# Output rows made token by token: nine products in one bank, attention's last, and the bias added to the input rows by GpSimd

## What is computed

```python
# x: (4, 1024, 128), 16 heads of 8; everything in float32
xn = layernorm(x)
attn = softmax(causal(rope(q) @ rope(k).T / sqrt(8))) @ v          # q, k, v = xn @ Wqkv
y = attn @ Wproj                                                   # "proj"
# product-key experts: per token 4 heads, 8 best of 8 x 8 pairs out of 512 experts
w = silu(xn @ down_embed[idx]) * softmax(scores)                   # as a dense (tokens, 512) matrix "coef"
experts = w @ up_embed
mlp = (silu(xn @ Wg + bg) * (xn @ Wu + bu)) @ Wd + bd
out = x + y + experts + mlp
```

## Time and profile before

| | us |
|---|---|
| median of 3 runs | 773.35 (772.94 to 777.92) |
| the profiled execution | 770.89 |
| its span, first to last instruction | 769.1 |
| mean granted TensorE clock | 0.955 of 2.4 GHz |

### The profile page before, as it was taken

One profiled execution on the slowest core, in us unless ns is written; L12 is line 12 of the kernel. 1 busy time (PEld: TensorE's weight loads), 2 busy tenths in 40 slices (PEclk: granted clock), 3 DMA queues, 4 the chain that ended last, 5 costly groups with the idle time before them and its releaser, 6 DMA issues.

```text
span 769.1 us, 16962 instructions
## 1 busy us (share of the span) xinstructions
PE 669.6 (87%) x5788; PEld 296.0 (38%) x5788; DVE 639.9 (83%) x1369; ACT 538.3 (70%) x811; POOL 492.9 (64%) x588
## 2 busy tenths in 40 slices
PE   4847678899899898999889999999989998899896
PEld 3523234333334343443334344433334344343332
DVE  3238789998899989998999989997899989988741
ACT  3523435568876786678867786778867786769794
POOL 6413676777765866767656865877656765558570
PEclk9766959999999999999999999999999999999999
DMA  8322400011140000022130000022120000000100
GB/s 158 99 82 67 84 2 22 2 64 63 66 110 2 3 1 23 1 68 93 43 98 3 16 2 1 22 75 79 50 71 2 17 2 2 17 1 3 30 1 14
DMA packets 29115, 29.93 MB, mean 39 GB/s; under 512 B 5730, under 2 KB 27202, under 8 KB 27458
## 3 DMA queue, kind: packets, MB, share of 16 engines
q1 hardware_dynamic: 25832, 27.66, 12.4%
q10 hardware_dynamic: 3200, 1.18, 0.7%
HBM read 18.81 MB, written 8.39 MB: 35 GB/s over the span
## 4 chain that ended last, share of the span: by engine, by line
DVE 37%; PE 36%; issue 15%; POOL 7%; ACT 2%; DMA 2%; DVEq 0%; ACTq 0%; POOLq 0%
DVE pmax L868 17%; PE ybank L996 7%; PE ring L1081 5%; DVE ssum L790 5%; PE ring L973 4%; PE ring L948 4%; PE ring L1071 4%; POOL coef L633 3%; PE ring L1002 3%; PE ring L1035 3%; DVE coef L797 2%; PE ring L1063 2%; DMA xin<-in_L_attn_x 2%; POOL coef L637 2%; PE ring L1056 2%
## 5 line engine op out<-in xcount | busy, mean ns | idle before, releaser
L868 DVE TENSOR_REDUCE pmax<-ring 128x2 f32<-128x1024 f32 (+3 forms) x304 | 342.7, 1158 | 38.2 <-PE ring L958 29.5
L756 ACT ACTIVATE pT<-ring 128x1024 f32<-128x1024 f32 (+3 forms) x384 | 297.6, 809 | 105.8 <-PE ring L980 67.9
L633 POOL TENSOR_TENSOR coef<-coef,ssum 128x512 f32<-128x512 f32 x128 | 171.1, 1353 | 147.1 <-DVE ssum L790 147.1
L996 PE MATMUL ybank<-pT,vaug 128*32 128x512 f32 (+3 forms) x1536 | 151.6, 498 | 0.6 <-ACT pT L756 0.5
L973 PE MATMUL ring<-qs,ks 59*128 59x512 bf16 (+3 forms) x768 | 123.1, 335 | 25.6 <-DVE pmax L868 14.0
L948 PE MATMUL ring<-ks,qs 56*128 56x512 bf16 (+3 forms) x768 | 113.9, 340 | 32.3 <-DVE pmax L868 17.3
L606 POOL TENSOR_TENSOR ssum<-sim 128x512 f32<-128x512 f32 x128 | 131.5, 1059 | 0.0
L717 ACT ACTIVATE coef<-ssum,nbest 128x512 f32<-128x512 f32 x128 | 88.3, 716 | 18.1 <-DVE coef L802 8.0
L973 PEld LDWEIGHTS ring<-qs,ks 59*128 59x128 bf16 x768 | 40.4, 93 | 144.9 <-ACT pT L756 44.6
L790 DVE TENSOR_SCALAR ssum<-ssum,best,zinv 128x512 f32<-128x512 f32 x128 | 83.7, 686 | 2.0 <-ACT coef L717 1.9
L948 PEld LDWEIGHTS ring<-ks,qs 56*128 56x128 bf16 x768 | 37.0, 95 | 109.3 <-DVE pmax L868 44.1
(11 more groups left out here) (119 smaller groups left out, 865.0 us busy)
## 6 DMA issues: line engine op xcount, KB each, us to landing
parts_scratch<-parts SPq DMA_DIRECT2D x16, 384.0 KB, 2.5
qs<-parts_scratch SPq DMA_DIRECT2D x16, 192.0 KB
ks<-parts_scratch SPq DMA_DIRECT2D x16, 192.0 KB
xin<-in_L_attn_x SPq DMA_DIRECT2D x8, 256.0 KB, 8.9
qs<-parts_scratch SPq DMA_DIRECT2D x16, 128.0 KB
ks<-parts_scratch SPq DMA_DIRECT2D x16, 128.0 KB
rows<-in_L_attn_x SPq DMA_DIRECT2D x8, 256.0 KB, 7.0
out<-rows SPq DMA_DIRECT2D x8, 256.0 KB, 7.2
```

What stands on the lines that cost most here:

```text
L633: g.tensor_tensor(coef4[:, h, :], coef4[:, h, :], ssum[:, h, :], ALU.mult).then_inc(weighed, 1)
L756: a_.activation(pT[:, n % NPT, 2 * pr:2 * pr + 2, q0:CHUNK], pair_of(t)[:, :, q0:CHUNK], ACT.Exp, scale=SCALE).then_inc(ring_copied_scalar, 1)
L868: v.tensor_reduce(pmax[:, it, k0 // CHUNK, 2 * pairs[0]:2 * pairs[-1] + 2] .rearrange("p (j e) -> p e j", e=2), pair_of(t)[:, :, 0:w * len ...
L996: ins = t_.matmul(ybank[32 * j:32 * j + 32, q0:CHUNK], vaug[:, b % 2, kt, v0:v0 + 32], pT[:, n % NPT, j, q0:CHUNK], start=kt == 0, stop=kt ...
```

## The change

1. `mlp` has nine parts, all with the activations stationary and the weights moving: part k is four products of 128 tokens each, into the four quarters of the bank. Parts 0 to 3 use `hT`, 4 to 7 `gT`, and part 8 is attention's `yT` with `wproj_sb`. The bank is held until part 8.
2. `proj` and `outT` are gone, with `oT`, ACT's bias operation and DVE's first addition. DVE adds the bank to `rows` once.
3. The bias is loaded broadcast over the partitions (`bd_rows`), and a new POOL task, `lift`, adds it to `rows` after their load. DVE's addition waits for it.
4. `hT` and `gT` come free by a new semaphore (`dense_used`) that part 7 raises, no longer by the bank's last fill.
5. `SEQUENCE` is another string, again of 2048 tasks.

```diff
-    "spread": each(B, NT, RH), "keep": each(B, NT, RH), "mlp": each(B, NC, 2 * NF),
+    "spread": each(B, NT, RH), "keep": each(B, NT, RH), "mlp": each(B, NC, 2 * NF + 1),
...
-TASKS.update({k: each(B, NC) for k in ("rows", "yT", "proj", "outT", "store")})
+TASKS.update({k: each(B, NC) for k in ("rows", "lift", "yT", "store")})
...
-load_parts sim top best max*2 cand dif load zinv max weights scores spread*2 keep*2 scores pairs spread weigh
-rows scores cand max sim values keep pairs scores spread load max*2 keep dif top values scores*3 max*3 scores
-best values scores ycopy weights max scores values max coef scores*2 zinv spread ln spread*2 values*2 negate
...
-values*3 scores*4 values rows values*2 ycopy mlp y mlp yT proj outT store
...
+negmaxT load_parts negmax third load_parts sim top best max cand max dif max zinv keep weights rows spread
+scores load spread pairs keep weigh spread scores sim spread lift cand load keep scores max keep values pairs
+scores dif max*2 top scores values scores*2 max*2 best scores*3 max*3 scores ycopy scores coef weights spread
...
+values*2 experts y mlp scores*3 mlp*2 scores*3 values*3 scores*3 values scores values*2 lift ycopy mlp y mlp yT
+mlp store
...
-                (bd_sb[:, :], bd.rearrange("(p a) -> p a", a=1)),
+                (bd_rows[:, :], bd.rearrange("(a d) -> a d", a=1).to_broadcast([P, D])),
...
+                elif kind == "lift":
+                    c, k = t[2], b * NC + t[2]
+                    pool.wait_ge(rows_loaded[k % 2], 16 * (k // 2 + 1))
+                    if k == 0:
+                        pool.wait_ge(weights_loaded, 16 * NLATE)
+                    g.tensor_tensor(rows[:, k % 2, :, :], rows[:, k % 2, :, :],
+                                    bd_rows[:, :].unsqueeze(1).to_broadcast([P, TPC, D]), ALU.add).then_inc(rows_ready, 1)
...
-                elif kind == "mlp" and t[3] == 2 * NF - 1:
-                    filled(act, t)
-                    if (b, t[2]) != (0, 0):
-                        filled(act, ("outT", b, 0) if t[2] else ("outT", b - 1, 1))
-                    a_.activation(oT[:, :], bank, ACT.Identity, bias=bd_sb[:, 0:1])\
-                        .then_inc(ring_copied_scalar, 1)
...
-                elif kind == "proj":
-                    c = t[2]
-                    copied(dve, ("mlp", b, c))
-                    filled(dve, t)
-                    v.tensor_tensor(oT[:, :], bank_of(t), oT[:, :], ALU.add).then_inc(ring_copied_vector, 1)
-                elif kind == "outT":
-                    c, k = t[2], b * NC + t[2]
-                    dve.wait_ge(rows_loaded[k % 2], 16 * (k // 2 + 1))
+                elif kind == "mlp" and t[3] == 2 * NF:
+                    k = b * NC + t[2]
+                    dve.wait_ge(rows_ready, k + 1)
                     filled(dve, t)
                     v.tensor_tensor(rows[:, k % 2, :, :], bank_of(t).rearrange("p (n d) -> p n d", d=D),
                                     rows[:, k % 2, :, :], ALU.add).then_inc(ring_copied_vector, 1)
...
-                        pair = wd_sb[:, k, :], hT[:, k, :]
-                    else:
+                        of, w = hT[:, k, :], wd_sb[:, k, :]
+                    elif k < 2 * NF:
                         if k == NF:
                             copied(pe, ("experts", b, (c + 1) * TPC - 1))
-                        pair = up_sb[:, k - NF, :], gT[:, k - NF, :]
-                    ins = t_.matmul(bank, pair[0], pair[1], start=k == 0, stop=k == 2 * NF - 1)
-                    if k < 2 * NF - 1:
+                        of, w = gT[:, k - NF, :], up_sb[:, k - NF, :]
+                    else:
+                        copied(pe, ("yT", b, c))
+                        of, w = yT[:, :], wproj_sb[:, :]
+                    for n in range(TPC):
+                        ins = t_.matmul(bank[:, n * P:(n + 1) * P], of[:, n * P:(n + 1) * P], w,
+                                        start=(k, n) == (0, 0), stop=(k, n) == (2 * NF, TPC - 1))
+                    if k < 2 * NF:
+                        if k == 2 * NF - 1:
+                            ins.then_inc(dense_used, 1)
                         continue
...
-                elif kind == "proj":
-                    copied(pe, ("yT", b, t[2]))
-                    ins = t_.matmul(bank, wproj_sb[:, :], yT[:, :], start=True, stop=True)
-                elif kind == "outT":
-                    copied(pe, ("proj", b, t[2]))
-                    ins = four(bank, lambda n: oT[:, n * P:(n + 1) * P])
```

More of the change, by code:

```diff
@@ L116 @@
[L116 to L164, removed]
-scores*2 first turned experts proj sim keep*2 xT third scores max values scores second max*2 y outT swapped max
@@ new lines @@
+values ln values negate scores values total spread zinv spread xn weigh negmaxT keep spread cand y experts max
+keep sim values coef keep*2 scores pairs top scores*2 max*3 scores max negmax scores max*2 best ycopy values*2
+scores max dif ln rot xT scores weights max*2 spread total xn swapped turned rest spread*2 values keep_parts
+first spread values max*3 third load_parts zinv scores rot second weigh swapped xT max turned keep turned scores
+max*2 scores v keep*2 scores keep experts max*3 rest first values sim scores top y scores max swapped second
@@ new lines @@
+negmax scores max*2 total values coef ycopy first best scores swapped scores*2 rot y max*2 keep_parts turned
+cand max*2 spread max dif spread weights zinv negate third v keep*2 values*2 scores rest scores max experts
+negmaxT spread mlp max spread keep sim pairs ycopy values weigh values keep max*2 coef scores mlp cand mlp top
+max scores*2 total mlp dif keep_parts rot scores max values load_parts scores load_parts pairs best negmax
+experts weights second zinv first y max scores mlp spread rest max mlp scores spread weigh max*2 coef mlp max*2
@@ new lines @@
+weights turned keep_parts max scores zinv spread third values*2 negate scores ycopy max pairs rest keep scores
+sim negmaxT v max weigh max keep spread values*2 spread keep*2 scores*3 y scores max scores load_parts max
+values*2 rot keep_parts ycopy load_parts scores*2 y max*2 coef values total cand top first rest mlp scores
+second scores max mlp experts mlp dif scores best max mlp spread max*2 scores pairs mlp zinv mlp keep max*2
+weights spread keep scores second values*3 spread scores max keep scores mlp max spread scores max mlp
@@ new lines @@
+scores rot total ycopy spread negmax swapped up max keep_parts spread rest spread xn keep spread scores weigh
+values third first turned experts keep*3 mlp sim xT coef y scores*3 second max values scores load_parts max lift
+scores swapped turned max*2 rot turned cand values*2 negmax ycopy scores v scores rest scores top first scores
+total dif up y best swapped second experts max scores max values first swapped rot scores spread max*2 values
+weights turned keep_parts zinv spread scores*2 third max scores values*2 max scores max pairs negate ycopy sim v
@@ new lines @@
+scores rest keep max weigh max negmaxT values keep spread values spread scores keep*2 scores*2 y load_parts
+scores max scores values*2 rot scores keep_parts ycopy max scores mlp max*2 load_parts coef values total cand
+top first rest second scores*2 dif mlp y experts best mlp max scores max mlp spread max*2 pairs mlp zinv scores
+mlp keep max*2 weights spread keep scores second values*3 spread scores max keep scores mlp max scores max mlp
+scores max spread keep_parts sim scores third weigh keep top down*3 yT down store max third scores values best
```

130 lines of the change are left out of this document (78 added, 52 removed).

## The result

| | before | after |
|---|---|---|
| median of 7 runs, us | 773.13 (771.75 to 777.92) | 782.86 (781.15 to 787.03) |
| ratio to before | | 1.0125 (95%: 1.0094 to 1.0156) |
| span of the profiled execution, us | 769.1 | 779.8 |
| mean granted TensorE clock | 0.955 | 0.958 |

The changed kernel is 9.7 us slower, and the clock is not the reason: what was granted is the same within 0.003. The forecast was 775.5 with a range of 765 to 783, most of the chance on no measurable change. The time lies at the upper edge of the range, and on the side that had 0.20.

What follows compares the result with a forecast made beforehand. PE and DVE were taken to bound the kernel in lockstep, no single engine setting the time. Terms -3.5 - 1.6 + 0.7 + 6 + 1 = +2.6 us gave 773.5 on the profiled execution, 775.9 on the median, rounded 775.5; range 765 to 783.

Steps and rivals of the forecast that it cites:

- The first lift: Chunk 0's `lift` waits on POOL for the load of `rows`, idle 8 to 10 us: +6 us, bounds 0 and 9.
- Rival B: The wait of chunk 0's `lift` costs nothing at the end (early load or later slack): 770 us, chance 0.27.
- the other seven lifts: Later `lift` tasks on POOL stand 40 or more places behind a load SP can issue early; no wait there.
- The tail: Last chunk: part 8 takes `proj`'s place and DVE's `rows` follows at once: -1.6 us, counted in full.
- Matmuls: PE: products of 4 x 128 cost 0.03 us more each, +2 us over 72; `oT` transposes go, -4; net -2.
- Rival E: PE's weight loads do not hide under running products: 83 us over 72 products, 805 us or more, chance 0.02.
- POOL: Eight `lift` operations of 1.15 us, 9.2 us; by POOL's 7% of the chain +0.7 us, bounds 0 and 9.2.
- What of the saving reaches the end: DVE's 4.8 and PE's 1.4 us outside the last chunk, by chain shares 2.3, in full 6.2; taken 3.5.
- The ring: Bank held for 44% of the order, not 20%; tight fills 350 to 429: bounds 0 and +7 us, taken +1.
- C: Held bank makes each tight fill cost 0.09 us: 781.5 us, chance 0.16; sign: PE's waits for maxima 38 us or more.
- A: The forecast itself: a small saving, eaten by the wait of chunk 0's `lift`: 775.5 us, chance 0.42.
- D: PE's and DVE's savings count in full, ACT's makes room for `scores`, first wait hidden: 763.5 us, chance 0.11.

Runs made afterwards that it cites:

- the two-bank form in the old order: Changed kernel's operations in the previous kernel's order, part 8 given its own bank, DVE adding both banks to `rows`, lifts before `weigh`: 774.99 us, ratio 1.0031.

## Why the prediction was right in parts and short in sum

**The sum.** -3.5 - 1.6 + 0.7 + 6 + 1 = +2.6 was forecast, +9.7 measured. That 782.86 lies inside the stated range, by 0.1 us, is luck: the cost of the order and of the hold was missed, and the saving of the operations taken too small, which hid part of it. By step:

**The first lift.** Right in place, mechanism and size. The load landed at 92.8 (forecast 92.1), POOL stood still 9.9 us (8 to 10), the statistics at 98.53 (98.1), the price at the end 5.6 us (6). For `cand` the prediction gave 94.1, but by its own sum the lift ends at 93.3, where `cand` starts; 94.1 is where `best` can follow. Measured are 93.99 and 94.80. Rival B falls with it: later slack did not take it back. The sentence on the other seven lifts misread the string: lift 2 stands at place 640, 23 places ahead of its load at 663. No wait came of it, because SP had issued that load at 251.99, ahead of the lift at 276.29.

**The tail.** -1.6 forecast, -1.6 in the trace.

**Matmuls.** +0.03 us a product, right: 0.99 us each, in the kernel after too. Weight loads on the same rows of the array do overlap. Rival E falls. The Trainium skill's sentence on row groups (TensorE: Matmul & The Clock Gate; it stands under "The mechanism" there, not under the heading that the prediction names) would have a weight load on the same rows wait for the running product; the trace after does not agree with it either: 0.99 us for a product with its eight loads, each of which lasts 0.19 us.

**POOL.** A lift takes 1.27 us and not 1.15, and the length of eight cost 2.5 us (0.4 to 4.6), where 0.7 was forecast. Six of them moved cost 7.7 us, and so the step that failed is "by its 7% of the chain". The share of a chain tells how much of the path lies on an engine now, not what one more operation does at its place. At one place it costs 0.6 us, at another 4 us.

**What of the saving reaches the end.** The step "count by the engines' shares of the chain", -3.5 with -1.6 for the tail, was probably too small taken alone. At one order and nearly one assignment of banks (846 of the 984 fills that both have wait for the same earlier copies), the old operations with the bank withheld stand at 1.0136 and the new ones with the first lift late at 1.0052: 0.84%, 6.5 us less, give or take 2, and without most of the lifts' length (1.0020) 9 us, against 5.1 forecast. Part of this may be the place that I gave `outT` there.

**The ring.** The term, +1, failed in its kind, not only in size. Counting tight fills and giving each a price (+7 at most, +1 taken) supposes that a held bank costs by itself. In the old order 72 tight fills cost 17 us, in the new one 39 cost between 0 and 6. The waits from which the price was taken, 31.3 us, rose to no more than 34.4 where 17 us were lost. The lower bound, PE's high busy share in the stretches in which the bank is held, told nothing either: these stretches were made for the bank being away.

**The order.** The step that is missing from the sum. I set the new string at nothing, because I took the tasks to have moved by few places, which was a wrong count: 166 of them moved by more than 10. It costs the old operations 7.5 us (4.6 to 10.4). Put together from the measured steps: new order and hold +10.5 (1.0136), new operations with their lifts -6.5, the first wait +5.6: 9.6. That these three add up is no check, because each ratio starts where the one before ends; each step has 2 to 3 us of uncertainty.

**The rivals.** C, slower, ended nearest (781.5), and its sign came, 47.9 us of waits for the maxima against the 38 set for it. But most of these waits belong to the first lift (37.0 without it), and at this order the hold costs 0 to 6 us by itself. The larger part of what A lacked, 7.5 us, is in the order, which no rival had. D fell.

**What stays open.** Why the new order is poorer for the steps around 270 to 290, 480 to 530 and 620 to 700 us was not taken apart. Nor was it tried whether the two-bank form in the old order, with its lifts behind `coef`, is faster than the kernel before: it stood at 1.0031 with the lifts in the poor place, so it may be.

## What to carry to other kernels

When a new operation waits for a transfer on an engine that works in order, work out when that transfer is issued on its queue and landed, and follow what stands behind the waiting operation: here that forecast 6 us and 5.6 (3 to 8) were measured. In a kernel whose two busiest engines are near 90% and whose order is written out, do not price a moved operation, a held buffer or a reshuffled order by shares or by counts; a change to either cost between nothing and 2% here, and no count of tight fills told it ahead. Before you set a new order at nothing, count by how many places each task moved, kind by kind. Put a filler operation behind the last step of the chain that others wait for, not into the largest wait of the table.

## What the hardware showed that I had not expected

Nothing of an engine's speed, but one thing on its way of working. POOL's largest wait (`weigh` for DVE's `keep`, 147 us in the kernel before) is a sum over 72 waits, and ahead of single tiles it is zero: an operation of 1.30 us put there moved the whole chain, and behind it the shift grew by three times its length. And an instruction that issues a DMA can itself take long on SP's queue: the last of the four copies took 2.95 us and the load of `rows` behind it 2.76, against 0.37 to 0.51 for the same loads of `rows` later on. The four copies ahead of that load, from 74.51 to 80.34, moved it by 5.8 us.
